# A transformer layer on eight cores: the weight loads of its last stages are issued at their place of use instead of ahead of it

## The reference, cut to what matters

```python
x = x + attn(layernorm(x))        # 16 heads of 64, sin(30 * q k / 8) instead of softmax
x = x + ffn(layernorm(x))
def bitlinear(x, w):              # one scale for each row of w
    scale = clip(mean(abs(w), axis=1), 1e-5, None)
    w = clip(round(w / scale), -1, 1) * scale
    return x @ w.T
h = bitlinear(x, w_fc) + gate * (x @ v.T @ fast_b.T @ u.T)     # w_fc: 4096 x 1024, rank 16
ffn = bitlinear(relu(h) ** 2, w_proj)                          # w_proj: 1024 x 4096
```

## Time and profile before

| | us |
|---|---|
| median of 4 runs | 7173.14 |
| lowest and highest run | 7163.88 and 7197.02 |
| the profiled execution | 6673.02 |
| its span on core 3, the slowest | 6671.5 |
| spans of all cores | 6601.9 to 6671.5 |

### The profile page before, as it was taken

How to read it: one execution, slowest core, us unless ns; L and a number is a source line. 1 busy time by engine, 2 the same in 40 slices (tenths; PEclk the granted TensorE clock), 3 DMA queues, 4 the chain that set the end, 5 groups by cost and what they waited for, 6 DMA issues and landing times.

```text
span 6671.5 us, 62656 instructions; the slowest of 8 cores (6601.9 to 6671.5 us)
## 1 busy us (share of the span) xinstructions
PE 4534.8 (68%) x23298; PEld 1784.8 (27%) x23298; DVE 1634.6 (25%) x2564; ACT 1386.3 (21%) x2440; POOL 159.3 (2%) x120
## 2 busy tenths in 40 slices
PE   2566667775777776577777577777437776667773
PEld 1322222322223222232322223232213332223331
DVE  2211111122111112211112211111554344444342
ACT  2122232220232331123232032323320000000000
POOL 1000000000000000000000000000110000000000
PEclk7688887877999998899999799999759888889885
DMA  3110010001000001100000200000220000000002
GB/s 119 71 32 29 29 38 32 33 7 71 37 13 26 13 13 45 57 26 13 26 13 7 82 26 18 21 26 1 101 77 20 18 17 27 27 26 20 20 17 98
DMA packets 50860, 232.04 MB, mean 35 GB/s; under 512 B 7975, under 2 KB 12091, under 8 KB 42380
## 3 DMA queue, kind: packets, MB, share of 16 engines
q1 hardware_dynamic: 50028, 225.94, 9.6%
q0 software_dynamic: 544, 2.10, 0.1%
HBM read 194.33 MB, written 33.69 MB: 34 GB/s over the span
## 4 chain that ended last, share of the span: by engine, by line
PE 57%; DVE 13%; ACT 10%; DMA 9%; issue 6%; POOL 2%; ACTq 1%; DVEq 1%; SPq 0%; POOLq 0%
PE ps L651 13%; PE ps L669 9%; PE ps L1151 7%; PE ps L555 5%; PE ps L598 5%; PE ps L1111 5%; ACT FA L689 4%; ACT FA L691 4%; PE psT L213 3%; PE ps L484 3%; PE ps L766 3%; DVE FA L718 2%; DVE FA L714 2%; DMA HA<-fmspill 2%; PE ps L1161 1%
## 5 line engine op out<-in xcount | busy, mean ns | idle before, releaser
L651 PE MATMUL ps<-FA 128*64 128x512 f32 x2048 | 1167.0, 653 | 357.0 <-ACT FA L691 357.0
L689 ACT ACTIVATE FA<-ps 128x512 f32<-128x512 f32 x1024 | 613.9, 599 | 3021.0 <-PE ps L674 3020.6
L655 PE MATMUL ps<-FA 128*64 128x512 f32 x2048 | 1181.9, 661 | 0.0
L669 PE MATMUL ps<-HA,H 64*128 64x512 bf16 x3072 | 850.6, 398 | 440.2 <-DVE FA L718 385.0
L674 PE MATMUL ps<-HA,H 64*128 64x512 bf16 x3072 | 855.0, 400 | 0.0
L714 DVE TENSOR_TENSOR FA<-FA,ps 64x512 f32<-64x512 f32 x224 | 152.1, 679 | 2067.9 <-PE ps L655 2067.9
L691 ACT ACTIVATE FA<-ps 128x512 f32<-128x512 f32 x1024 | 612.7, 598 | 0.0
L669 PEld LDWEIGHTS ps<-HA,H 64*128 64x128 bf16 x3072 | 238.4, 96 | 1315.8 <-issue 1169.9
L1111 PE MATMUL ps<-H 128*128 128x512 bf16 x2048 | 484.8, 398 | 131.5 <-DVE FA L1186 59.8
L213 PE MATMUL psT<-idn,H 128*128 128x128 bf16 x1280 | 150.9, 306 | 575.2 <-DVE H L404 183.5
L1151 PE MATMUL ps<-HA,H 128*128 128x512 bf16 x2048 | 490.1, 395 | 25.3 <-POOL xvb_lo L1137 19.1
(11 more groups left out here) (149 smaller groups left out, 3037.8 us busy)
## 6 DMA issues: line engine op xcount, KB each, us to landing
HA<-fmspill SPq DMA_DIRECT2D x40, 2048.0 KB
FA<-wproj SPq DMA_DIRECT2D x32, 1024.0 KB
fmspill<-HA SPq DMA_DIRECT2D x8, 2048.0 KB, 6.7
FA<-wfc SPq DMA_DIRECT2D x14, 1024.0 KB
FA<-x_own SPq DMA_DIRECT2D x2, 4096.0 KB
FA<-x_own SPq DMA_DIRECT2D x8, 1024.0 KB
FA<-x_oth SPq DMA_DIRECT2D x16, 512.0 KB
FA<-x_oth SPq DMA_DIRECT2D x8, 1024.0 KB
```

What stands on the lines that cost most here:

```text
L651: s_=first, t_=last: e.matmul(b[0:64, :], f_V(k)[:, pc_ * 128: pc_ * 128 + 64], f_attn(o), start=s_, stop=t_, tile_position=(0, 0)))
L655: o=bufB_, s_=first, t_=last: e.matmul(b[64:128, :], f_V(k)[:, pc_ * 128 + 64: pc_ * 128 + 128], f_attn(o), start=s_, stop=t_, tile_positi ...
L669: k=kt, q=qt, s_=(pi == 0), t_=(pi == 2): e.matmul(b, K_(pc_)[0:64, k * 128:(k + 1) * 128], Q_(pc_)[0:64, q * 512:(q + 1) * 512], start=s_ ...
L689: p.ins("scalar", lambda e, b=zA["ap"], o=bufA: e.activation(out=f_attn(o), in_=b, func=AF.Sin, scale=1.0))
```

## The change

- `prep_weight("q", ...)` of group g > 0 stands at the start of group g instead of between the last block and the output product of group g-1. The load of the output bias (once) waits for two semaphores instead of three.
- The 16 pieces of the w_proj scale pass stand in a loop of their own behind the slab loop and the zeroing, instead of two in each turn of the slab loop. The order of waits inside the pass is the same.
- x v.T stands behind that pass, copied from PSUM by VectorE and split by two GpSimd instructions over 16 x 2048, instead of being formed during the slab loop and split by VectorE.
- The gated product x v.T fast_b.T stays on chip instead of being stored to HBM and read back for each quarter.
- `prefetch_fc` and the two GpSimd-issued loads of w_fc are gone. Each half of each block loads its 256 rows of w_fc at the top of the block into the one buffer `f_w0`, takes absolute values in one ScalarE instruction of 128 x 2048 into `f_w1`, sums them with two VectorE reductions, and derives the thresholds there.
- Five waits of VectorE on its own semaphore (in the Q, K and squared-ReLU code) become drains.

```diff
     for g in range(G):
+        if g > 0:
+            prep_weight("q", g, 0, slab_tg, wt_tg)
+            slab_tg = p.val("T")
         wprep_vg = p.val("V")
...
-        if g < G - 1:
-            prep_weight("q", g + 1, 0, kt_tg, kt_tg)
-
...
         c0b_tg = p.val("T")
-        scale_iter(2 * sl)
-        scale_iter(2 * sl + 1)
-        if sl % 2 == 1:
-            lr_banks.append(emit_lr(sl // 2, x2l))
     x2t_v = p.val("V")
...
+    for i in range(16):
+        ec, hf = i // 2, i % 2
+        Lb = spj_L[i % 2]
+        if i == 0:
+            w = (("V", spl3),)
+        else:
+            w = (("S", sq_prev),)
+        ld = dma(Lb, wpj_h[ec * 128:(ec + 1) * 128, hf * 2048:(hf + 1) * 2048],
+                 waits=w)
+        p.wait("scalar", "dL", ld)
...
+            p.wait("scalar", "V", red_prev)
+        sq_prev = p.ins("scalar", lambda e, b=Lb: e.activation(
+            out=spj_O, in_=b, func=AF.Abs, scale=1.0 / FF), "S", 1)
+        p.wait("vector", "S", sq_prev)
...
+    p.wait("gpsimd", "V", vv)
+    hv = p.ins("gpsimd", lambda e: e.tensor_copy(out=h2_xvhi(), in_=f_xvf()), "G", 1)
+    p.wait("gpsimd", "G", hv)
+    gv = p.ins("gpsimd", lambda e: e.tensor_tensor(
+        h2_xvlo(), f_xvf(), h2_xvhi(), ALU.subtract), "G", 1)
...
     for jb in range(NJB):
+        for hb in range(2):
+            ld = dma(dst3(f_w0(), 1024),
+                     rows3(wfc_h, jb * 512 + hb * 256, 2, 1024),
+                     waits=(("S", p.val("S")), ("V", p.val("V"))))
+            p.wait("scalar", "dL", ld)
+            sq = p.ins("scalar", lambda e: e.activation(
+                out=f_w1(), in_=f_w0(), func=AF.Abs, scale=1.0 / D), "S", 1)
+            p.wait("vector", "S", sq)
             for j in range(2):
+                c = jb * 4 + hb * 2 + j
+                p.ins("vector", lambda e, c_=c, j_=j: e.tensor_reduce(
+                    sm["sfc_m"][:, c_:c_ + 1],
+                    f_w1()[:, j_ * 1024:(j_ + 1) * 1024],
+                    AX.X, ALU.add), "V", 1)
...
         for tq in range(NQT):
-            ldq = dma(xvb_f, xvb_h[:, tq * 512:(tq + 1) * 512],
-                      waits=(("dS", xvb_w[-1]), ("G", xvb_g[0])), sem="dS")
-            p.wait("gpsimd", "dS", ldq)
+            p.wait("gpsimd", "V", xvb_v)
...
-        if jb + 1 < NJB:
-            prefetch_fc(jb + 1, rbv)
         emit_proj(NQT - 1, hi_s, lo_v)
```

More of the change, by code:

```diff
@@ L25, in __init__ @@
         self.q = {e: [] for e in ENGINES}
-        self.cnt = {s: 0 for s in ("dL", "dS", "dG", "T", "V", "S", "G")}
+        self.cnt = {s: 0 for s in ("dL", "dS", "T", "V", "S", "G")}
         self.sems = {}
@@ L725, in build_nc @@
             kt_tg = p.val("T")
[L727 to L728 removed]
         if g == 0:
[L731 to L732 removed]
+            bo_ld = dma(f_bo(), bo_h, waits=(("T", slab_tg), ("S", p.val("S"))))
             p.wait("tensor", "dL", bo_ld)
@@ L794, in build_nc @@
     ha_free_t = p.val("T")
[L795 to L848, removed]
     c0b_tg = ha_free_t
-    vv = None
-    lr_banks = []
     for sl in range(8):
@@ L883, in build_nc @@
                     first = False
-                x2l = tbatch(srcs, HA[:, base + tt * 1024: base + (tt + 1) * 1024],
-                             idn)
+                tbatch(srcs, HA[:, base + tt * 1024: base + (tt + 1) * 1024], idn)
         c0b_tg = p.val("T")
-        scale_iter(2 * sl)
-        scale_iter(2 * sl + 1)
-        if sl % 2 == 1:
-            lr_banks.append(emit_lr(sl // 2, x2l))
     x2t_v = p.val("V")
[L893 to L929, removed]
     spill_v = spill_tiles[-1]
@@ L948, in build_nc @@
                                                       0.0, ALU.mult, ALU.add), "V", 1)
-    p.wait("tensor", "V", vv)
-    xvb_w = []
+    p.wait("tensor", "V", x2t_v)
+    for tq in range(NQT):
+        stx = pool.acquire()
+        n_mm = [0]
+        txv = None
+        for (vhl, xhl) in ((0, 0), (1, 0), (0, 1)):
+            vT = sm["vT_hi"] if vhl == 0 else sm["vT_lo"]
+            for dc in range(DC):
+                n_mm[0] += 1
+                fn = lambda e, b=stx["ap"], v_=vT, d=dc, x_=xhl, q=tq, \
+                    first=(n_mm[0] == 1), last=(n_mm[0] == 24): e.matmul(
+                    b[0:16, :], v_[:, d * 16:(d + 1) * 16],
+                    seg_rhs(X2T_HI if x_ == 0 else X2T_LO, q * 4, 4, d),
+                    start=first, stop=last)
+                if n_mm[0] == 24:
+                    txv = p.ins("tensor", fn, "T", 1)
+                else:
+                    p.ins("tensor", fn)
+        p.wait("vector", "T", txv)
+        vv = p.ins("vector", lambda e, b=stx["ap"], q=tq: e.tensor_copy(
+            out=f_xvf()[:, q * 512:(q + 1) * 512], in_=b[0:16, :]), "V", 1)
+        pool.release(stx, "V", vv)
+    p.wait("gpsimd", "V", vv)
[3 more added lines that the diff above has]
+        h2_xvlo(), f_xvf(), h2_xvhi(), ALU.subtract), "G", 1)
+    p.wait("tensor", "G", gv)
     for tq in range(NQT):
@@ L1014, in build_nc @@
-    xvb_g = [0]
+        pool.release(stx, "V", vv)
+    xvb_v = p.val("V")
     r2_tg = p.val("T")
     for jb in range(NJB):
-        if r2_tg is not None:
-            p.wait("vector", "T", r2_tg)
-            r2_tg = None
-        for pr in (0, 1):
-            if pr == 1:
-                p.wait("vector", "T", tb_tv[0])
-            for j in range(2):
-                jt = pr * 2 + j
-                c = jb * 4 + jt
-                p.ins("vector", lambda e, j_=j, c_=c, pr_=pr: e.tensor_scalar(
-                    h2_a(j_), (f_w0() if pr_ == 0 else f_w1())[:, j_ * 1024:
-                                                               (j_ + 1) * 1024],
+        for hb in range(2):
[6 more added lines that the diff above has]
+            p.wait("vector", "S", sq)
+            for j in range(2):
+                c = jb * 4 + hb * 2 + j
[3 more added lines that the diff above has]
+                    AX.X, ALU.add), "V", 1)
+            c0 = jb * 4 + hb * 2
+            p.ins("vector", lambda e: e.drain())
+            p.ins("vector", lambda e, c_=c0: e.tensor_scalar(
+                sm["sfc_c"][:, c_:c_ + 2], sm["sfc_m"][:, c_:c_ + 2], 1e-5, 0.0,
+                ALU.max, ALU.add))
+            p.ins("vector", lambda e: e.drain())
+            p.ins("vector", lambda e, c_=c0: e.tensor_scalar(
+                sm["thp_fc"][:, c_:c_ + 2], sm["sfc_c"][:, c_:c_ + 2], 0.5, 0.0,
+                ALU.mult, ALU.add))
+            p.ins("vector", lambda e, c_=c0: e.tensor_scalar(
+                sm["thn_fc"][:, c_:c_ + 2], sm["sfc_c"][:, c_:c_ + 2], -0.5, 0.0,
+                ALU.mult, ALU.add))
+            p.ins("vector", lambda e: e.drain())
+            if r2_tg is not None:
+                p.wait("vector", "T", r2_tg)
+                r2_tg = None
+            for j in range(2):
+                c = jb * 4 + hb * 2 + j
+                p.ins("vector", lambda e, j_=j, c_=c: e.tensor_scalar(
+                    h2_a(j_), f_w0()[:, j_ * 1024:(j_ + 1) * 1024],
@@ L1170, in build_nc @@
             p.wait("vector", "T", fcb[-1][2])
-            p.wait("vector", "S", p.val("S"))
+            if hi_s:
+                p.wait("vector", "S", hi_s)
             rbv = None
@@ L1203, in build_nc @@
             p.wait("vector", "T", r2g)
-            p.wait("vector", "V", rbv)
+            p.ins("vector", lambda e: e.drain())
             for (jc, stf_, tf_) in fcb:
@@ L1255, in build_nc @@
     p.wait("sync", "dS", p.val("dS"))
-    p.wait("sync", "dG", p.val("dG"))
     with (
```

113 lines of the change are left out of this document (35 added, 78 removed).

## The result

| | before | after |
|---|---|---|
| ratio of the runs that compare, 95% interval | 1 | 1.0236 [1.0219, 1.0254] |
| spans of the cores in the profiled execution, us | 6601.9 to 6671.5 | 6772.7 to 6804.9 |
| time of the profiled execution, us | 6673.02 | 6806.57 |

The change makes the kernel 2.4% slower, which is 157 us of the 6635.5 to 6647.0 us that the comparable runs of before took. The four runs of before that stood ahead of the prediction (median 7173) take no part in the ratio: their cores are not on record, but later executions of before of that length (7097 to 7243 us) all show at least one die at a mean granted clock of 0.74 to 0.78, where an undisturbed one has 0.88.

A forecast was written before the change was run, and what follows sets the result against it. TensorE's delays were taken to bound attention, single-file waits the layernorm stage and FFN block borders. Middle 58.7 plus lost prefetch 123.1 gave +182 us, taken as +190 on 7173: 7363, range 7310 to 7415 (0.72).

The forecast's parts named there:

- Base: Whole kernel: +182 us against the profiled 6673.0, taken as +190 on the 7173 median, since everything may be 7.5% slower there.
- Q weights: Attention, start of groups after the first: the 13.5 us of load and transposes stay on the path, net 0, 2 us either way each.
- Drains: Q, K and squared-ReLU evictions: drains in place of self-waits cost 0, 2 us either way.
- Slab loop: Slab loop before the FFN: turns fall from 17.85 to 10.65 us, as the two scale pieces leave.
- Scale pass: w_proj scales behind the zeroing: 14 pieces at 7.8 us, load 5.9 then \|w\| 1.91, 109.2 us; bounds -13 and +7.
- x v.T on GpSimd: Behind the w_proj scales: matmuls hidden, four copies 2.5 us, GpSimd's two operations over 16 x 2048 taken as 6.5 us.
- w_fc at its use: Top of each FFN block: each half exposed for 10.1 us; losing the prefetch costs 20.2 + 70.7 + 32.2 = 123.1 us.
- Gated product: Kept on chip: about 8 us of stores gained in the middle stage; FFN reloads about 0, at most -16.
- Clock given back: Rival: longer idle stretches raise the granted clock elsewhere, giving about 7210 (no change, 0.04) or 7085 (faster, 0.02).
- Loads that collide: Rival: all eight cores load w_fc at once, 5 us more on each of 30 exposed loads, 7510; chance 0.12 above 7415.
- Only the prefetch: Rival: middle stage comes out even, only the lost prefetch costs, +123 to +133, 7300; no chance of its own.
- Loads that run ahead: Rival: scale loads use both buffers freely, a piece costs 1.91 + 2.28 + 0.2 instead of 7.8, giving 7315; chance 0.10.

## Why the prediction came out as it did

- **Sign and order.** Right by its own steps. The forecast sum was +182 us against the profiled execution, measured are 157 by the ratio and 157 by the stage table. In the two stages where the change works the forecast was 71.1 + 113.0, measured are 58.2 + 105.5. The range, in ratios to its own base of 7173 (1.019 to 1.034), holds 1.024.
- **Base.** The step from 182 to 190, which scaled the loss for the 500 us that the median lay above the profile, was wrong. Executions that take part in the ratio lie near the profiled one, and the loss in them is 157, further from 190 than from 182. The row to be trusted was the profiled execution; only as a ratio can the forecast be held against the result.
- **Q weights: 0.** Confirmed in kind (13.7 against 13.5 us, moved).
- **Drains: 0.** Nothing contradicts it: the gap between the K evictions went from 0.10 to 0.07 us, and the stages stayed.
- **Slab loop.** 10.65 us a turn forecast, 10.5 measured.
- **Scale pass: the mis-sized term.** 14 pieces at 7.8 us were 109.2; the trace has 4837.15 to 4935.15, 98.0, at 7.0. I took the 5.94 us from |w| to |w| in the earlier trace rows as the load's duration. On the changed kernel's core 7 it takes 4.74 to 5.04 and its hand-overs 0.1, as the w_fc load of the earlier trace rows did, the row that I used as lower bound only. The 5.94 were a property of the core that I read: on core 0 of the same execution the same wait is 4.97 us (last section). This is 11 of the 13 us by which the middle was too high: forecast 243.5 (4777.2 to 5020.7), measured 230.6; the rest is mostly in the slab loop and the zeroing, which were done 2 us sooner than forecast. From the fit that the Trainium skill gives for loads issued by GpSimd (DMA: Bandwidth & Descriptors, "Anatomy of one DMA — SWDGE (gpsimd) path") follows an estimate of 4.4 us for 1 MB. These loads, issued by SP, lie 0.3 to 0.6 us above it, and the two w_fc loads that GpSimd issued in the kernel before landed after 5.5 us (median).
- **x v.T on GpSimd.** Forecast 6.5, measured 1.89 + 4.05 = 5.9. Its matmuls did run beside the zeroing and the pass.
- **w_fc at its use.** 10.1 us a half forecast; 9.96 from issue to comparison in the first half, 10.1 from last copy to comparison in the second. The first half's net price was forecast as 27.2 less 20.8 and 22.9, 32.2 us in all; measured are 26.9 less 23.1 in the mean of all borders, 26.5 us in all. FFN forecast +113, measured +105.5 and, alone, +110 and +111.
- **Gated product.** Forecast 8 us of stores, measured 5.5.
- **Rivals.** Clock given back: refuted by TensorE's 1130 us in both FFN windows and the lower mean clock. Loads that collide: at 5 us more for each load refuted. From issue to |w| it takes 5.0 us in the median of the scale pass and 4.9 for w_fc, on all cores of the changed kernel; single loads are longer, up to 6.6 and 6.1. Only the prefetch (an even middle stage): refuted by the +58.2 of that stage. Loads that run ahead: not so in the changed kernel, and where I made them run ahead the price of a piece was 5.0; the 4.4 that the rival gave held for the first few alone.

## What to carry to other kernels

A wait that stands in an engine's list ahead of unrelated work delays that work too, whichever engine is busy most: here a prefetch placed just ahead of the last projection saved 10 us in one half of a block and only about 4 in the other. Before a transfer is moved, ask for each place what ends the wait there; and price a load by rows of more than one core, in which the engine waited for nothing else. If the median of the runs is far from the profiled execution, don't scale by it.

## What the runs showed of the hardware that was not expected

The same 1 MB w_proj load took 5.94 us on core 3 of the kernel before, from the end of one |w| to the start of the next, and 4.97 to 5.08 in the changed kernel's pass. The slab loop's other work is not the reason. On core 0 of the same execution that work is the same, and the wait is 4.97 us (4716.57 to 4721.54):

```profile
4714.66 1.91 ACT L823 ACTIVATE FA<-FA 128x2048 f32<-128x2048 f32 x1 [9.77 <-DVE spj_h L827]
4721.54 1.91 ACT L823 ACTIVATE FA<-FA 128x2048 f32<-128x2048 f32 x1 [0.56 <-DMA FA<-wproj]
```

The time is lost between issue and data. Windows behind the issue, of before on core 3 (issued at 4792.88) and of after on core 7 (issued at 4844.03), end with the DMA share and GB/s:

```profile
4792.88:4794.60 1.72, 0.00 (x0) 0.00 (x0) 1.69 (x1) 1.72 (x2) 0.00 (x0) 0.50 0.00 0
4844.03:4844.90 0.87, 0.00 (x0) 0.00 (x0) 0.84 (x1) 0.00 (x0) 0.00 (x0) 0.50 0.00 0
```

By the packets in the traces the first one starts 1.80 us behind the issue on core 3 and 0.95 on core 7; from there the megabyte takes 3.62 and 3.59 us, so it moves equally fast. In this stage of before about half of the loads of cores 3, 4 and 6 start 1.5 to 2.2 us behind their issue, on core 3 those that the |w| then waits for; nearly all of the other five cores start within 0.9 to 1.1. What holds them back on some cores was not tried.
